# Two graph-attention networks on one core: loads of the next stage moved ahead of the stage's end, two tiles by halves, scores as extra columns

## The reference

```python
# network 0: three convolutions on x1, then an output projection
x1 = relu(x @ W_ah + b_ah)
def gat(x, W, a_src, a_dst, b, heads):          # one convolution
    h = (x @ W).reshape(N, heads, C)
    s = leaky_relu((h * a_src).sum(-1)[src] + (h * a_dst).sum(-1)[dst], 0.2)
    p = exp(s - segment_max(s, dst)[dst])
    alpha = p / (segment_sum(p, dst)[dst] + 1e-16)
    return segment_sum(alpha[:, :, None] * h[src], dst) + b
node = concat([relu(gat(x1, W_i, ..., heads=4, C=192)) for i in range(3)])
x2 = layernorm(x + relu(node @ W_out + b_out))
# network 1: two convolutions
h = elu(gat(x2, W1, ..., heads=4, C=512))       # 2048 features
y = gat(h, W2, ..., heads=1, C=768)
out = layernorm(x2 + y)
```

## Time and profile before

| | |
|---|---|
| median of 3 runs | 2026.57 us (2025.38 to 2027.65) |
| the profiled execution's own time | 2024.48 us |
| its span in the trace | 2022.8 us |
| TensorE busy (matmuls) | 1839.7 us, 91% of the span |
| VectorE, ScalarE, GpSimd busy | 1446.6, 1022.3, 135.5 us |
| mean granted TensorE clock, share of full | 0.956 |

### The profile page before, as it was taken

How to read it: one execution, slowest core, us unless ns; L and a number is a source line. 1 busy time by engine, 2 the same in 40 slices (tenths; PEclk the granted TensorE clock), 3 DMA queues, 4 the chain that set the end, 5 groups by cost and what they waited for, 6 DMA issues and landing times. The chain is left out here.

```text
span 2022.8 us, 30487 instructions
## 1 busy us (share of the span) xinstructions
PE 1839.7 (91%) x11278; PEld 1768.4 (87%) x11278; DVE 1446.6 (72%) x2470; ACT 1022.3 (51%) x1621; POOL 135.5 (7%) x131
## 2 busy tenths in 40 slices
PE   6998899994999999986999899969999995999898
PEld 5777699994999999985999789969999995999898
DVE  6877669996988988954555339547888885346756
ACT  3555421215798898854121322247788883232533
POOL 5110022200000000000100011100000000000000
PEclk9999899996999999997999899979999997999889
DMA  4221244335274436508544646462442405645302
GB/s 120 62 64 51 66 139 134 104 89 143 75 190 99 117 86 142 140 14 229 183 151 126 161 137 186 139 178 67 130 136 68 131 31 158 173 107 130 104 9 77
DMA packets 182075, 234.76 MB, mean 116 GB/s; under 512 B 76203, under 2 KB 155139, under 8 KB 181692
## 3 DMA queue, kind: packets, MB, share of 16 engines
q1 hardware_dynamic: 173957, 205.36, 36.8%
q0 software_dynamic: 7216, 24.91, 4.2%
q10 hardware_dynamic: 768, 2.70, 0.4%
HBM read 167.89 MB, written 65.03 MB: 115 GB/s over the span
## 5 line engine op out<-in xcount | busy, mean ns | idle before, releaser
L1007 PE MATMUL p_o<-h_in,p 125*125 125x193 f32 x2400 | 398.9, 328 | 25.4 <-DVE p L966 20.9
L1007 PEld LDWEIGHTS p_o<-h_in,p 125*125 125x125 f32 x2400 | 392.9, 188 | 28.5 <-DMA h_in<-h_rows 21.2
L923 ACT ACTIVATE e<-uv,col 125x1250 f32<-125x1250 f32 x240 | 299.2, 1346 | 18.1 <-DMA uv<-uv_rows 14.9
L1566 PE MATMUL p_o<-p_hi,h_parts 125*128 125x416 f32 (+1 forms) x960 | 282.6, 355 | 25.6 <-DVE p_lo L1500 19.4
L1566 PEld LDWEIGHTS p_o<-p_hi,h_parts 125*128 125x128 f32 x960 | 181.7, 189 | 31.8 <-issue 19.6
L961 DVE TENSOR_TENSOR e<-e 125x1250 f32<-125x1250 f32 x120 | 174.3, 1452 | 30.6 <-ACT e L923 30.5
L688 DVE CUSTOM_DVE_ANT_0 max_junk<-src_row,G 125x1250 bf16<-125x1250 f32 x120 | 180.9, 1576 | 8.9 <-DMA src_row<-score_rows 8.2
L775 PE MATMUL p_h<-pw_hi,x1T 128*125 128x384 f32 x720 | 186.1, 339 | 0.0
L966 DVE SCALAR_TENSOR_TENSOR p<-e,CT 125x1250 f32<-125x1250 f32 x120 | 175.3, 1461 | 4.2
L1303 PE MATMUL p_h<-pw_hi,x2T 128*125 128x256 f32 x960 | 174.9, 284 | 0.0
L1566 PE MATMUL p_o<-p_lo,h_parts 125*128 125x416 f32 (+1 forms) x480 | 169.8, 354 | 0.0
(11 more groups left out here) (245 smaller groups left out, 3491.5 us busy)
## 6 DMA issues: line engine op xcount, KB each, us to landing
f_raw<-turned SPq DMA_DIRECT2D x40, 500.0 KB
h_rows<-h_out SPq DMA_DIRECT2D x32, 560.0 KB
h_parts<-h_rows SPq DMA_DIRECT2D x40, 448.0 KB
uv<-uv_rows SPq DMA_DIRECT2D x24, 546.9 KB
turned<-out_f SPq DMA_DIRECT2D x18, 625.0 KB
G<-turned SPq DMA_DIRECT2D x20, 562.5 KB
h_rows<-h_out SPq DMA_DIRECT2D x24, 424.4 KB
h_in<-h_rows SPq DMA_DIRECT2D x24, 424.4 KB
```

The lines of the kernel that those rows point to most:

```text
L923: last = a.activation(e[:, g % RING, kind, :], uv[:, hh, kind, :], ACT.Exp, bias=col_src[kind][:, bass.ds(i * 2 + hh, 1), s])
L1007: last = nc.tensor.matmul(p_o[:, b, n * 256:n * 256 + C0 + 1], p[:, g % RING, d * T:(d + 1) * T], h_in[:, hh, s, 0:C0 + 1], start=(s == 0 ...
L1566: last = nc.tensor.matmul(p_o[:, bank(n, c), 0:w], h[:, s, kind, cols].bitcast(F32R), pp[:, g % RING, 0:w], start=(s == 0 and j == 0), sto ...
```

## The change

- **First heads.** `project` transposes and stores u and v of heads 0 to 3 early in its last iteration, and SP loads head 0's u, v and h in the middle of that iteration into room kept over the stage's end (`first_room`, which the raw weights had held). `aggregate_layer0` starts on them. In layer 1, SP loads head 0's u and v during unit 6 of `project_layer1`, into the ring that x2 had.
- **Last stores.** `aggregate_layer0` and `aggregate_layer1` no longer wait for their last stores; their semaphores live on, and the next stage waits for them just ahead of the first load that reads late rows.
- **More loaded ahead.** `aggregate_layer0` loads the first halves of tiles 0 and 1; `aggregate_layer1` loads the same of its successor and the first four parts of its weights.
- **Two tiles by halves.** Both output projections go through tile 0 first half, tile 1 first half, tile 0 second half, tile 1 second half, then tile by tile. The layer-1 one (now `project_out_layer1`) rounds the first weight parts and features of half 1 while half 0 still runs.
- **Scores as columns.** In `project_layer1` the 8 score vectors are columns 256 to 263 of unit 0's weights. DVE copies them out of each tile; one transpose of the source scores, two tiles after the last, replaces the separate product, and ACT stores the rows from it.

The core of the diff (left out: buffers moved into rooms that outlive a stage, semaphores renamed, and the rest of the rewritten loops):

```diff
+            def load_first_head():
+                uv, h = first_head_of_layer0(core)
+                sp.wait_ge(split_done, 2 + 2 * iters)
+                sp.wait_ge(first_stored, 32)
+                load_uv(sp, core, 0, uv, core.first_uv_in)
+                for part_no in range(2):
+                    sp.wait_ge(h_stored[part_no], 64 * per)
+                load_head(sp, h_rows, 0, h, core.first_h_in)
+
             def store(i, heads_to_load):
 
                 for u in range(2):
+                    if i == iters - 1 and u:
+                        load_first_head()
                     for part_no in range(2):
                         wait_apart(sp, h_kept, i * (2 * NT) + (NT * u + NH * (part_no + 1) + 4))
...
+                        if (i, u, t) == (iters - 1, 0, 4):
+                            act.wait_ge(first_turned, 1)
+                            a.activation(turned_first[:], p_s[0:HG * NT, 0:2 * T].rearrange("p (a q) -> p a q", a=2), ACT.Copy).then_inc(first_kept, 1)
+                            act.wait_ge(first_kept, 1)
+                            for kind in range(2):
+                                act.dma_start(core.uv_rows[kind, 0:HG * NT, :], turned_first[:, kind, :]).then_inc(first_stored, 16)
                         if t % NH == 0:
...
+                if i == iters - 1:
+                    pe.wait_ge(max_steps, 4)
+                    for kind, col in enumerate((u_col, v_col)):
+                        last = nc.tensor.transpose(p_s[0:HG * NT, kind * T:(kind + 1) * T],
+                                                   col[:, 0:HG, :].rearrange("p h t -> p (h t)"), ident[0:T, 0:T])
+                    last.then_inc(first_turned, 1)
...
             def load(i):
                 for s in range(2):
-
+                    if (i, s) == (0, 0):
+                        continue
                     wait_apart(sp, exp_ready, i * STEPS + (s + 1) * NT)
                     wait_apart(sp, p_used, i * STEPS + (s + 1) * NT)
-                    head = i * 2 + s
...
+            for t in range(2):
+                sp.dma_start(f_ahead[:, t], turned_rows[t, :, 0:KO // 2, :]).then_inc(ahead_in, 16)
             store(ITERS - 2)
             store(ITERS - 1)
-            for c in range(CW):
-                sp.wait_ge(stored[c], 16 * (1 + ITERS))
-            sp.wait_ge(ahead_in, 16 * (W_AHEAD + 1))
+            sp.wait_ge(ahead_in, 16 * (W_AHEAD + 2))
 
...
+                        if g == 0:
+                            wait_apart(act, core.first_uv_in if first else uv_in[0], 64 if first else i * 64)
+                        else:
+                            wait_apart(act, uv_in[1], i * 64 + 64)
...
+                        sp.wait_ge(uv_stored, 32)
+                        sp.wait_ge(x_turned, 2 * NT)
+                        load_uv(sp, core, 0, first_uv_of_layer1(core), core.first_uv_in)
             for part in range(2):
                 sp.wait_ge(h_stored[part], 64 * UNITS)
...
                 dve.wait_ge(h_rounded, n + 1)
+                if q == 0:
+                    v.tensor_copy(score[:, :, :, t], p_h[:, n % 4, HALF1:HALF1 + R].rearrange("p (a h) -> p a h", a=2)
+                                  ).then_inc(score_kept, 1)
                 v.tensor_tensor(h_out[:, t // NH, t % NH, 1, :], p_h[:, n % 4, 0:HALF1],
                                 h_out[:, t // NH, t % NH, 0, :].bitcast(F32), ALU.subtract).then_inc(h_split, 1)
...
-            def scores():
-                pe.wait_ge(wa_split, 1)
-                pe.wait_ge(x_split, 2 * NT)
-                for b, (at, n) in enumerate(CH):
-                    for k in range(KD):
-                        for j, (wp, xp) in enumerate(((wa_hi, xT[0]), (wa_hi, xT[1]), (wa_lo, xT[0]))):
-                            last = nc.tensor.matmul(p_r[0:R, b, 0:n], wp[:, k, :], xp[:, k, at:at + n],
-                                                    start=(k == 0 and j == 0), stop=(k == KD - 1 and j == 2))
-                last.then_inc(rows_summed, 1)
-
             def turn_scores():
-                pe.wait_ge(rows_kept, 1)
...
+                width = HALF1 + (R if q == 0 else 0)
                 for k in range(KD):
                     for j, (xp, wp) in enumerate(((xT[0], w_hi), (xT[0], w_lo), (xT[1], w_hi))):
-                        last = nc.tensor.matmul(p_h[:, n % 4, 0:HALF1], xp[:, k, at], wp[:, q % 2, k, :],
+                        last = nc.tensor.matmul(p_h[:, n % 4, 0:width], xp[:, k, at], wp[:, q % 2, k, 0:width],
                                                 start=(k == 0 and j == 0), stop=(k == KD - 1 and j == 2))
                 last.then_inc(h_summed, 1)
...
+                if n == NT + 1:
                     turn_scores()
...
+            sp.dma_start(core.w_first[:], w_next[0].rearrange("(k p) c -> p k c", p=128)[:, 0:K1 // 2, :]).then_inc(core.w_first_in, 16)
+            for s in range(2):
+                for c in range(CW):
+                    sp.wait_ge(stored[s][c], 16 * (ENDS // 4))
+            for t in range(2):
+                sp.dma_start(core.f_raw[:, t], turned_rows[0:K1 // 2, :, t * T:(t + 1) * T].rearrange("k p n -> p k n")).then_inc(core.f_first_in, 16)
             for c in range(CW):
                 store(ENDS - 1, c)
...
+    PIECES = ((0, 0), (1, 0), (0, 1), (1, 1)) + tuple((t, kh) for t in range(2, NT) for kh in range(2))
+    LAST = [PIECES.index((t, 1)) for t in range(NT)]
...
+            def load_f(n):
+                t, kh = PIECES[n]
+                sp.wait_ge(f_lo_done, n - 1)
+                sp.dma_start(f_raw[:, n % 2], turned_rows[t, :, kh * KH:(kh + 1) * KH, :]).then_inc(f_in[n % 2], 16)
 
             def load_x(t):
                 if t >= SLOTS:
...
-                    load_f(1, 0)
-                if k == 13:
+                if k == 12:
+                    load_f(3)
+                if k == 14:
                     load_x(0)
-            load_f(1, 1)
             load_x(1)
             for t in range(2, NT):
-                load_f(t, 0)
+                load_f(2 * t)
                 if t >= 3:
                     store(t - 3)
                 load_x(t)
-                load_f(t, 1)
+                load_f(2 * t + 1)
                 if t == 3:
                     sp.wait_ge(w_split, KO)
...
+            for part in range(PARTS // 2, PARTS):
+                load_w(0, part)
+            for stored in core.turned1_stored:
+                for of_chunk in stored:
+                    sp.wait_ge(of_chunk, 16 * (3 * H1 // 2))
+            load_f(2)
+            dma_in_two(sp, b_row, bias.rearrange("(o f) -> o f", o=1).broadcast_to([T, D]), bias_in)
+            for m in range(3, 2 * ALL):
+                load_f(m)
+                if m == 5:
...
+                    act.wait_ge(core.w_first_in, 16)
+                else:
+                    act.wait_ge(w_in[part], 16 * half + (16 if part >= PARTS // 2 else 0))
+                if half:
+                    act.wait_ge(piece_used, ALL - 1 if part < PARTS // 2 else ALL)
+                a.activation(w_hi[:, part * KP:(part + 1) * KP, 0:CW], raw(part), ACT.Copy).then_inc(w_rounded, 1)
+
+            def round_f(m):
+                if m < 2:
+                    act.wait_ge(core.f_first_in, 32)
+                else:
+                    act.wait_ge(f_in[m % 2], 16 * (m // 2))
+                    act.wait_ge(piece_used, m - 1)
+                a.activation(f_hi[:, m % 2], f_raw[:, m % 2], ACT.Copy).then_inc(f_hi_done, 1)
+
+            for half in range(2):
+                first = half * ALL
...
+            for half in range(2):
+                first = half * ALL
+                for part in range(2, 4):
+                    rest_of_w(half, part)
+                rest_of_f(first + 1)
+                for part in range(4, 6):
+                    rest_of_w(half, part)
+                rest_of_f(first + 2)
+                for part in range(6, 8):
+                    rest_of_w(half, part)
+                rest_of_f(first + 3)
+                leave(half, 0)
+                beside(half, 1)
+                for t in range(2, NT):
...
+                        rest_of_f(first + 2 * t + kh)
+                    leave(half, t - 1)
+                    beside(half, t)
+                if half == 0:
+                    rest_of_f(ALL)
+                    rest_of_w(1, 0)
+                    rest_of_w(1, 1)
+                leave(half, NT - 1)
```

565 lines of the change are left out of this document (289 added, 276 removed).

## The result

The changed kernel takes 1971.47 us, median of 4 runs (1969.66 to 1977.44), where the kernel before took 2025.97 us in the same session: ratio 0.9738, 95% interval 0.9714 to 0.9762. The forecast was 1969, range 1960 to 1986. The profiled execution took 1972.25 us and has a span of 1970.5 us, where my sum gave 1967.9 for the execution. All times and ratios are of fast executions; the only slow one, 3097.7 us at a mean granted clock of 0.557, was of experiment 4 and is left out there.

What follows compares the result with a forecast made beforehand. TensorE was busy 91% of the span, so the gain lay in its pauses and needless matmuls. Six places summed to -56.6 us from 2024.5, giving 1967.9, or about 1970 as a median; forecast 1969, range 1960 to 1986.

Steps and rivals of the forecast that it cites:

- Place 1: Opening of the first aggregation: exp waits only for the bias, not for u and v; -10.1 us.
- Place 2: First output projection: 6.9 us less store wait before it, 7.4 us less inside it; -14.3 us.
- TensorE waiting for weights: First output projection: 8.7 us of waits, of which 7.4 go and 1.3 stay for last block and fourth half.
- Place 3: Second projection: scores as eight extra columns instead of a separate product and its waits; -13.7 us.
- Place 4: Opening of the second aggregation: ACT's 3.2 us wait for u and v goes; -3.2 us.
- place 5: Second output projection's opening and half 0: first matmul 6.1 us sooner, half 0 4.5 us shorter; -10.6 us.
- So 4.5 goes: Half 0 of the second output projection: of 7.7 us over, 1.5 (clock) and about 1.7 (tile 3's features) stay.
- place 6: Turn from half 0 to half 1, second output projection: 3.23 us wait and 1.5 us lower clock go; -4.7 us.
- the weight stream: Rival: both output projections stay bound by weight loading, so 7.4 and 4.5 us come back: 1981 us; chance 0.20.
- The openings at places 1 and 4: Rival: ACT waits there for something hidden behind u and v; 5 and 1.7 us come back: 1976; chance 0.08.
- The clock: Rival: shorter pauses at four stage openings no longer lower the clock, 6 us more goes: 1963; chance 0.06.
- The 264 columns: Rival: second projection's 264-column matmuls leave the fast fp32r form, +59 us (2029) to +139 us (about 2110); chance 0.03.

Runs made afterwards that it cites:

- experiment 4: Changed kernel with the first output projection tile by tile and only that tile's first feature half loaded ahead: 1978.99 us, ratio 0.9782 to the kernel before.
- the trace again: Trace of the same changed kernel, without an edit, in a later session: 1972.39 us, ratio 0.9743 to the kernel before.
- experiment 5: Changed kernel with the 54 matmuls of the old separate score product put back, unread, in the second projection: 1983.20 us, ratio 0.9790 to the kernel before.
- experiment 9: Changed kernel with the second output projection tile by tile and one feature half loaded ahead: 1982.33 us, ratio 0.9787 to the kernel before.
- Experiment 7: Changed kernel with half 1's eight weight parts loaded two by two behind feature halves of pieces 6 to 9: 1970.31 us, ratio 0.9731 to the kernel before.

## Why the prediction was right, and where its terms were off

**Place 1**: opening -10.4 as priced, to 0.1 us, in the trace and by undoing it. What I left at nothing, the maxima, took 11.60 us in the trace after and 9.88 in the trace again (8.4 to 11.6 over all programs with the change, 9.8 before), so a shift of half a microsecond there is neither shown nor excluded.

**Place 2**: priced -14.3, measured -6.6 for the pause and -6.4 for the stage (-6.9 in the trace again), so -13.2. The pause is right to 0.3 us, though undoing the store wait gives only 5.3. In the stage I called 8.7 us "TensorE waiting for weights". Counted start by start, the stage before had 5.4 us of such waits, and lower clock twice, 1.9 us at its start and 1.5 behind the longest stop (947.5 to 950.9). That second lower clock went with its stop, which is why the price held. What I left for the last block hardly appeared in these two traces (0.0 and 0.7 us of waits), but it did in others: in two of the seven further traces with this order and no added matmuls in this stage, of experiments 5 and 9, TensorE waits 1.4 and 1.6 us for weights there. The clock at the start cost 2.8 us in the first trace and 1.6 in the second instead of 1.5.

**Place 3**: priced -13.7, measured -14.0 to -15.1. The eight columns cost 3 ns, not 3.5. The lower clock behind the pause went along with it, and the price held it, since it fell into tile 10, whose copy ends the stretch that I had priced. Of the 15.1 in the first trace about 1 is the start of the stage: lower clock over 3.6 us of it there, over 8.7 before and 8.3 in the trace again.

**Place 4**: priced -3.2, measured -4.0. The 3.2 are ACT's wait; 0.1 is the bias, and the remaining 0.7 lies between the last product and the stage's first DMA. This pause came out between 15.5 and 16.1 us in the traces with the same code there, so up to 0.6 of the 0.7 can be scatter.

**Places 5 and 6**: priced -15.3, measured -6.3 and -6.3 (-6.7 again), so -12.8. The pause and the turn of the halves were right (6.1 said, 6.3 found; 4.7 said, 5.0 found in the trace and 5.3 to 5.7 by undoing). The term that was off is "So 4.5 goes": half 0 got only 1.3 to 1.7 us shorter (92.3 before, 91.0 and 90.6 now). Of the remainder I had put "about 1.7" on tile 3. It is a wait of 2.2 to 2.7 us and then 1.5 us of lower clock. I had seen the queue behind the eight weight parts and left out that a stop can bring its own lower clock, though I had priced just that at place 6. Experiment 7 removes both, and half 0 takes 86.8 us.

**The sum**: -56.6 said. The places give -9.3 - 13.2 - 14.6 - 4.0 - 12.8 = -53.9 (mean of the two traces), the medians -54.5 and -51.1. What differs elsewhere in the first trace, 3.4 us at the start and -2.0 at the end, lies in code that did not change. The end goes with its lower clock (7.2 us of the stage after, 14.9 before); at the start lower clock explains about half. The terms missed in both directions, too much at places 1, 2 and 5 with 6 (0.8, 1.1 and 2.5 us) and too little at 3 and 4 (0.9 and 0.8), so that the sum came as near as 2.7 us is in part luck.

**The rivals**: the first, the weight stream, gave back 7.4 us at place 2 and 4.5 at place 5. At place 2 it was mostly wrong: 6.4 to 6.9 us came, and waits for weights of up to 1.6 us are left in some traces. At place 5 some 3 of the 4.5 did not come, by the order of the loads, as experiment 7 shows, and not by their number. The openings at places 1 and 4 were not held by anything hidden. The clock did not come back sooner on the whole. The 264 columns stayed in the fast form.

## What to carry to other kernels

When a load is moved ahead of a stage, price its wait from the trace and look for what the next small wait is; here the small bias DMA was 2.0 us, and the opening shrank by the rest exactly. A stop of TensorE of 2.2 to 2.7 us cost 3.8 to 4.2 where lower clock followed it, and this holds for the stops that a change leaves as well. Lower clock did not always follow: in two of the nine traces with this stop (2.2 to 3.2 us), at 2.4 us each, it did not. A queue entry placed ahead of a load that is needed sooner costs what its own bytes take: here eight weight parts needed some 70 us later stood ahead of a feature half needed in 9.

## What the runs showed of the hardware

A shorter pause did not mean less lower clock behind it: ahead of the first output projection the pause went from 16.0 to 9.5 us, and the matmuls at the lower level lasted 3.7 us before, 6.0 after and 3.5 in the trace again. Filling pauses with matmuls raised the mean granted clock from 0.966 to 0.980 and moved the time by less than 0.3%: the first output projection gave the faster clock back in waits for weights, the first aggregation in a wait for ACT of 3.3 us where the changed kernel waits 0.8 and 1.6, and the second did not get shorter either. The length of a stop did not decide alone whether lower clock followed: it did after one of 1.4 us ahead of tile 10 in the trace before and after two of 0.9 and 1.0 us close together in experiment 4, and not after one of 1.4 us in experiment 5 (first output projection) nor after the two of 2.4 us at tile 3. And the same work reached `project` between 259.95 and 265.16 us, 5 us of scatter in a span of 1970 from that stretch alone. The same store of 640 kB, awaited at the same place in the program, took 6.9 us of waiting in the trace of one program and 5.2 in that of another.
